# Toeplitz blocks of a convolution: turned round on ScalarE after the load, or stored once in final order

## What is computed

```python
h = tok_ref(x, adjacencies, ids, ...)          # (64, 128, 192)
u = layernorm(h)
k = implicit_filter(128, w1, b1, w2, b2, w3, b3, freq, deltas)   # (128, 192)
y = fft_conv(u, k)                 # per channel: y[t] = sum over s <= t of k[t - s] u[s]
h = h + y + u * bias
h = h + moe(layernorm(h))          # 8 experts, the best 2 of each row
```

## Time and profile before

| | |
|---|---|
| median of 3 runs | 1166.27 us (1157.18 to 1166.58) |
| the profiled execution's span | 1296.4 us |
| PE busy in it | 963.5 us (74%) |
| DVE busy | 641.1 us (49%) |
| ACT busy | 543.3 us (42%) |
| POOL busy | 680.0 us (52%) |
| mean DMA rate | 113 GB/s |
| first stage | 0 to about 513 us |
| convolution | about 513 to 562 us |
| routing | to about 710 us |
| experts | to the end |

### The profile page before, as it was taken

How to read it: one execution, slowest core, us unless ns; L and a number is a source line. 1 busy time by engine, 2 the same in 40 slices (tenths; PEclk the granted TensorE clock), 3 DMA queues, 4 the chain that set the end, 5 groups by cost and what they waited for, 6 DMA issues and landing times.

```text
span 1296.4 us, 24517 instructions
## 1 busy us (share of the span) xinstructions
PE 963.5 (74%) x7442; PEld 736.7 (57%) x7442; DVE 641.1 (49%) x2223; ACT 543.3 (42%) x1323; POOL 680.0 (52%) x608
## 2 busy tenths in 40 slices
PE   1654445455546654958846999999999999999995
PEld 0533333333334433958746577777777777777774
DVE  1143444354443536378686355555454555555552
ACT  1121212122122223557556455555555565555552
POOL 6455554654556520025301267677667667667773
PEclk9966666666666766975569699999999999999998
DMA  6243435253525423930780353384385355333342
GB/s 196 74 133 114 160 86 179 73 169 93 164 73 180 131 73 108 285 97 1 217 263 9 99 114 51 51 231 96 64 239 120 51 118 120 49 49 53 50 52 29
DMA packets 119491, 146.24 MB, mean 113 GB/s; under 512 B 13475, under 2 KB 105798, under 8 KB 117414
## 3 DMA queue, kind: packets, MB, share of 16 engines
q0 software_dynamic: 39552, 53.26, 21.2%
q1 hardware_dynamic: 78902, 82.31, 20.8%
q10 hardware_dynamic: 1008, 10.34, 2.1%
HBM read 107.05 MB, written 38.82 MB: 113 GB/s over the span
## 4 chain that ended last, share of the span: by engine, by line
PE 51%; another core or an unknown queue 23%; DVE 8%; issue 5%; ACT 5%; DMA 4%; DVEq 2%; POOL 1%; SPq 1%; ACTq 1%; POOLq 0%
PE bank L582 6%; PE bank L715 6%; PE bank L711 6%; PE bank L730 5%; PE bank L732 5%; PE bank L731 5%; PE bank L712 3%; PE bank L714 3%; PE bank L713 3%; PE bank L618 2%; PE bank L694 2%; DMA out<-Hs,si 2%; ACT U L794 2%; PE bank L592 2%
## 5 line engine op out<-in xcount | busy, mean ns | idle before, releaser
L894 ACT ACTIVATE Hs<-bank,U 128x256 bf16<-128x256 f32 x426 | 204.5, 480 | 249.9 <-PE bank L715 236.8
L517 POOL DMA_INDIRECT out<-Hs,si x142 | 234.8, 1653 | 73.3 <-issue 50.7
L507 POOL DMA_INDIRECT blob<-xtab_d,gi x142 | 156.9, 1105 | 189.0 <-DVE gi L1207 151.7
L582 PE MATMUL bank<-ev_g,diag 128*12 128x192 f32 x384 | 95.7, 427 | 175.6 <-ACT diag L773 165.2
L1222 DVE TENSOR_TENSOR Hs<-Hs 128x512 bf16<-128x512 f32 x213 | 147.4, 692 | 139.6 <-ACT Hs L895 119.0
L476 POOL DMA_INDIRECT ev_g<-in_word_emb,idx x192 | 185.3, 965 | 58.5 <-issue 58.5
L730 PE MATMUL bank<-U,Hs 128*128 128x192 bf16 x852 | 210.6, 247 | 0.0
L732 PE MATMUL bank<-U,Hs 128*128 128x192 bf16 x852 | 208.9, 245 | 0.0
L731 PE MATMUL bank<-U,Hs 128*128 128x192 bf16 x852 | 208.7, 245 | 0.0
L895 ACT ACTIVATE Hs<-bank,U 128x256 f32<-128x256 f32 x426 | 205.3, 482 | 0.0
L582 PEld LDWEIGHTS bank<-ev_g,diag 128*12 128x12 f32 x384 | 43.9, 118 | 227.2 <-issue 119.0
(11 more groups left out here) (184 smaller groups left out, 1700.5 us busy)
## 6 DMA issues: line engine op xcount, KB each, us to landing
U<-blob_d SPq DMA_DIRECT2D x20, 771.0 KB
U<-blob_d SPq DMA_DIRECT2D x20, 672.0 KB
adj_s<-in_adj SPq DMA_DIRECT2D x48, 256.0 KB
ev_g<-kpad_d SPq DMA_DIRECT2D x24, 512.0 KB, 5.9
wst<-in_wsrc SPq DMA_DIRECT2D x8, 1344.0 KB
blob_d<-blob ACTq DMA_DIRECT2D x7, 1443.0 KB
xtab_d<-U SPq DMA_DIRECT2D x4, 1552.0 KB, 8.3
out<-Hs SPq DMA_DIRECT2D x4, 1536.0 KB, 10.5
```

The costliest lines, as they stand in the source:

```text
L507: pool.indirect_dma_start(xg_f[:, w, h, :], None, xtab_d, bass.IndirectOffsetOnAxis(ap=gi[:, w, h:h + 1], axis=0)).then_inc(xg_in[w], 16)
L517: pool.indirect_dma_start(out, bass.IndirectOffsetOnAxis(ap=si[:, p, h:h + 1], axis=0), yo[:, p, h, :], None, compute_op=ALU.add).then_inc ...
L582: last = mm(bank[3][0:KG, 0:D], diag[:, p, k, :], ev_g[:, p, j, b, :], start=k == 0, stop=k == KG - 1)
L894: f(hh[w][:, d, :], ps, ACT.Gelu, bias=bi[:, d:d + 1])
```

## The change

The reversal is taken out of the loads' path. The filter lies in forward time in columns 127 to 254 of `kT`, with zeros in 0 to 126 and 255, and the two tables made on the host are no longer reversed. As soon as `kT` is ready, ACT's queue issues 24 stores: each takes 8 partitions of `kT` (8 channels), from each 128 windows of 128 values that start one value further left with each s, and writes them to `toep_d`, laid out as (chunk, s, channel, t): the Toeplitz blocks in final order. `load_toep` then loads one block with 4 KB in a row for each partition. PE multiplies from `toep` directly and waits for `toep_in`; a ring buffer is loaded again after `conv`. The 24 turns on ACT are gone, and so are the two stores of `kpad_d`.

```diff
-        kpad_d = nc.dram_tensor("kpad_d", (D, NFFT), fp32).ap()
+        toep_d = nc.dram_tensor("toep_d", (NCH, 128, CC, 128), fp32).ap()
...
-            sp.wait_ge(kready, 2)
-            sp.dma_start(kpad_d[0:D0, :], kT[:, 0, :]).then_inc(kpad_stored, 16)
-            sp.dma_start(kpad_d[D0:D, :], kT[0:D1, 1, :]).then_inc(kpad_stored, 16)
-            sp.wait_ge(kpad_stored, 32)
+            sp.wait_ge(toep_stored, 16 * NCH)
 
             def load_toep(c, s):
-                src = bass.AP(tensor=kpad_d.tensor, offset=c * (CC * NFFT), ap=[[1, 128], [NFFT, CC], [1, 128]])
-                sp.dma_start(toep[:, s, :, :], src).then_inc(toep_in[s], 16)
+                sp.dma_start(toep[:, s, :, :], toep_d[bass.ds(c, 1), :, :, :].rearrange("a s c t -> (a s) c t")).then_inc(toep_in[s], 16)
...
-                    sp.wait_ge(turned, it * RING + s + 1 - RING)
+                    sp.wait_ge(conv, it * RING + s + 1 - RING)
...
-                pe.wait_ge(turned, c + 1)
+                pe.wait_ge(toep_in[s], 16 * (it + 1))
                 for k in range(CC):
                     n = 2 if k < CC - 1 else 1
-                    last = mm(bank[6 + s % 2][:, k * B:(k + n) * B], tp[:, s % 2, k, :],
+                    last = mm(bank[6 + s % 2][:, k * B:(k + n) * B], toep[:, s, k, :],
...
+            act.wait_ge(kready, 2)
+            for c, n in ((0, D0), (1, D1)):
+                for k in range(0, n, CC):
+                    shifted = bass.AP(tensor=kT, offset=k * 2 * NFFT + c * NFFT + S - 1, ap=[[2 * NFFT, CC], [-1, 128], [1, 128]])
+                    act.dma_start(toep_d[(c * D0 + k) // CC, :, :, :].rearrange("s c t -> c s t"), shifted).then_inc(toep_stored, 16)
+
...
-            def turn(it, s):
-                act.wait_ge(toep_in[s], 16 * (it + 1))
-                after(act, conv, it * RING + s - 1)
-                f(tp[:, s % 2, :, :], reverse(toep[:, s, :, :]), ACT.Copy).then_inc(turned, 1)
-
-            turn(0, 0)
-            turn(0, 1)
             normal(NQ - 1, 1)
-            for s in range(2, RING):
-                turn(0, s)
-            with act.Fori(1, NCH // RING) as it:
-                for s in range(RING):
-                    turn(it, s)
...
-            v.memset(kT[:, :, S:NFFT], 0.0)
+            v.memset(kT[:, :, 0:S - 1], 0.0)
+            v.memset(kT[:, :, 2 * S - 1:NFFT], 0.0)
```

More of the change, by code:

```diff
@@ L60, in repeat @@
             return bass.AP(tensor=ap.tensor, offset=ap.offset, ap=dims)
[L62 to L67, removed]
         def after(eng, semaphore, value):
@@ L208, in tower @@
         eid = sb("eid", [1, NT], i32)
-        tp = old_adj[:, 0:2 * CC * 128].rearrange("p (a c t) -> p a c t", a=2, c=CC)
         hot_p = wst[:, 0:2 * PICKS * 128].rearrange("p (a r n) -> p a r n", a=2, r=PICKS)
@@ L244, in tower @@
         filt_arg = sem("filt_arg")
-        kpad_stored = sem("kpad_stored")
+        toep_stored = sem("toep_stored")
         kready = sem("kready")
@@ L277, in tower @@
         toep_in = [sem(f"toep_in{s}") for s in range(RING)]
-        turned = sem("turned")
         conv = sem("conv")
@@ L954, in _ @@
             for c, n in ((0, D0), (1, D1)):
-                kk = kT[0:n, c, 0:S]
+                kk = kT[0:n, c, S - 1:2 * S - 1]
                 v.tensor_scalar(kk, bank[0][0:n, 256 + 128 * c:384 + 128 * c], filt[0:n, c, 1:2], 1.0 / NFFT, ALU.add, ALU.mult)
@@ L1271 @@
     w = 2.0 * np.pi * np.linspace(0.0, float(S - 1), S) / S
-    zT = np.stack([t, np.cos(1e-4 * w), -np.sin(1e-4 * w)]).astype(np.float32)[:, ::-1]
+    zT = np.stack([t, np.cos(1e-4 * w), -np.sin(1e-4 * w)]).astype(np.float32)
     r = np.arange(128, dtype=np.float32)
     cst = np.concatenate([np.eye(128, dtype=np.float32), (r[:, None] < r[None, :]).astype(np.float32),
-                          np.tile(np.arange(256, dtype=np.float32), (128, 1)), np.tile(t[::-1], (128, 1)), r[:, None],
+                          np.tile(np.arange(256, dtype=np.float32), (128, 1)), np.tile(t, (128, 1)), r[:, None],
                           (B * S + 1 + r[:, None] + 128 * (np.arange(NC) % 2)[None, :]).astype(np.float32),
```

## The result

The change makes the kernel slower: 1339.4 us (median of 4 runs, 1334.0 to 1348.0) against 1161.7 (4 runs), ratio 1.154, 95% interval 1.150 to 1.159. That is +177.7 us; +211.4 was forecast from a median of 1166.3.

A forecast was written before the change was run, and what follows sets the result against it. The first stage was taken as a chain of waits with ACT's `diag` in the loop. Release 263.1 less 49.8 gave 213.3 us delay; less 1.9 in the convolution, +211.4 on 1166.3 made 1377.7 us, range 1195 to 1450.

The forecast's parts named there:

- ACT's queue is held by the issues: First stage: store issues block ACT before the first `diag`, delaying all but two quads by 213.3 us; chance 0.56.
- The one issue of 2.44 us: Longest of four load issues on SP, median 0.38; taken as a sign that an issuer is held.
- The start and the reference: ACT's queue before the first quad: stores start at 38.7, `diag` otherwise at 49.8; delay is release less 49.8.
- The price: Time t of one 512 KB block's store on ACT's queue: 10.2 us, or 51 GB/s.
- The middle by ratio between 1/2 and 1/16: Store rate from eight partitions taken as 1/5.7 of full rate, giving 10.2 us a store.
- The lead of two blocks: On ACT's queue the issuer runs two blocks ahead, so about 22 of 24 must move before release.
- The convolution's 1.9 us: Convolution: PE's gaps and slower chunks go once the turns are removed, winning 1.9 us, 0.16% of the time.
- Carrying the delay over whole to the plain median: Whole kernel: +211.4 us from the 1296.4 us profile added unscaled to the plain median 1166.3, as queue held before the loop.
- unheld queue: Rival: ACT is not held, issues cost 8.2 us of idle time, total 1164 to 1167; chance 0.09.
- full rate: Rival: ACT is held but a store takes only 2.0 us, delay 32.9, total 1197; chance 0.07.
- Half the engines alone: Rival: ACT is held, stores use eight of sixteen engines, 4.0 us each, delay 76.9, total 1241; chance 0.20.
- even share per partition: Rival: eight source partitions get 8/128 of the rate, 28.8 us a store, delay 622, total 1787; chance 0.08.

The follow-up runs named there:

- stores_only: The kernel before with the change's 24 stores added on ACT's queue, its blocks still loaded from `kpad_d` and turned by ACT: 1344.2 us, ratio 1.157.
- spread_8: The changed kernel with the same 24 stores on ACT's queue, three for each pair of quads instead of all ahead of the first: 1183.8 us, ratio 1.018.
- conv_only: The changed kernel with one store left, every load reading that block (wrong result, same work): 1159.9 us against 1161.9 for the kernel before, ratio 0.996.

## Why the prediction was right, point by point

- **ACT's queue is held by the issues, and `diag` behind them stops everything.** Right. The single wait of GpSimd, 182.9 us, is the loss of 177.7 but for 5.2 us; `stores_only` has all of the loss. The one issue of 2.44 us was the trace's only warning, and it was enough.
- **The start and the reference.** I took 38.7 for the start and 49.8 for the first `diag`. Both come from the disturbed profile: undisturbed they are 23.8 and 29.3. And the loop does have slack, contrary to what I wrote: GpSimd is busy until 45.0, and it resumes 6.9 us after `diag`, so `diag` could start at 38.1 without loss. That the two errors nearly cancel is luck: 11.1 us assumed against 14.3 found between start and free time, 3.2 us.
- **The price.** 22 x 10.2 = 224.4 us were forecast for the time the queue is held; it was 197.2. This is the mis-sized term, 27 of the 38 us that the forecast was too high. The middle by ratio between 1/2 and 1/16 was a guess between two bounds, and no run shows the 1/5.7; measured were 8.2 us a store, 1/4.6 of the rate of 1.80 us a block. That the guess came within a quarter of the truth is in part luck. That few readers get more than an even share was put down without a row, and holds for the sources that were run: 8 neighbours had 64 GB/s, where 8/128 of the loads' 291 would be 18. The lead of two blocks was too long: by the records of single transfers 22.6 of the 24 blocks had moved when the last issue ended at 220.92, so ACT was 1.4 blocks ahead (1.6 at the end of `spread_8`). It hardly counts: 0.6 of a block is 5 us. The first two blocks, moved beside the gathers, took until 49.4, 12.8 us each, and the 20.6 after them 8.3 each.
- **The convolution's 1.9 us.** Right in the profiles, 47.5 or 48.0 to 45.6; the plain runs of `conv_only` have 1.9 between the medians. PE waited once for a load, 0.6 us.
- **Carrying the delay over whole to the plain median.** Right, though not for the reason given: the 130 us of difference lay in waits that one execution had.
- The sum again with measured terms: 227.9 - 45.0 = 182.9, less 5.2, is 177.7. Of the 5.2 the convolution explains 1.9 to 2.4; the rest was not traced and is within the scatter of four runs. The forecast's 38.3 us too many are 27.2 held queue, 3.2 start and slack, 4.6 from the median it started at, and a remainder of 3.3.
- **The rivals.** The unheld queue and the full rate fell in the first profile. Half the engines alone would have been 4 us a store and 1241 by the prediction's estimate, and 8.2 and 1339.4 were measured. Eight partitions spread out came to 3.0 and 1215.7, below that estimate; whether these stores were on half the engines was not shown. The even share per partition (28.8 us) fell.

## What to carry to other kernels

The issue of a transfer was not free work for the queue that it stood on: with 1.4 blocks of 512 KB waiting to move, a further issue lasted 8.2 us, as long as a block's transfer. So stores that nobody waits for belong on a queue, and at a place, where nobody waits for what is behind them. Before a transfer from few partitions is priced, look at which partitions: 8 neighbours gave 64 GB/s, 8 four apart 174. And ask first what the removed work cost the engine that sets the end, here 1.2 us of waiting for 25 us of ScalarE.

## What the runs showed that was not expected

- Eight neighbouring partitions as a source give 64 GB/s in 512-byte windows, whether these land 4 or 96 KB apart, and sixteen give 132. The last stores of `spread_8` moved at only 46.
- A profiled execution of the same kernel can be 130 us longer than another (1296.4 and 1159.8), all in the first stage, with late releases that the second does not have.
- SP's issues can be held by ACT's transfers too: in the changed kernel three adjacency loads that took 1.50 us to issue (the kernel before, at 49.93) took this long:

```profile
29.59 7.72 SPq L347 DMA_DIRECT2D adj_s<-in_adj  x3
```

The one store of `conv_only` is enough for it (0.40, 3.59 and 3.24 us from 29.61), and without it the second profile of the kernel before has 0.40, 0.45 and 0.46 at the same place. With partitions four apart they take 0.40, 1.54 and 0.46.
